# A graph-network kernel whose order is planned in Python: other durations and an occupancy in the planner, other buffers for the second sort, final rows kept in place

## The reference, cut to what matters

```python
x = _layernorm(x + _L0_gnn_ref(x, edge_attr_16, src, dst, ...))     # attention: softmax over a node's edges, sum of weighted rows
x = _layernorm(x + _L1_gnn_ref(x, edge_index, edge_weight, ...))    # attention, then normalise, MLP 64-128-64 with gelu, normalise
x = _layernorm(x + _L2_gnn_ref(x, edge_index, W, b))                # sums over src (row = src) of rows of dst, by degrees
x = _layernorm(x + _L3_gnn_ref(x, src, dst, edge_weight, 100000))   # sums over src of weighted rows of dst
```

## Time and profile before

| | us |
|---|---|
| median of three runs | 2920.24 |
| lowest, highest | 2912.45, 2922.75 |
| the profiled execution, device time | 2930.63 |
| its span in the profile | 2928.9 |
| PE busy | 2065.5 (71%) |
| POOL busy | 1644.4 (56%) |
| ACT busy | 1609.6 (55%) |
| DVE busy | 1599.0 (55%) |

### The profile page before, as it was taken

One profiled execution on the slowest core, in us unless ns is written; L12 is line 12 of the kernel. 1 busy time (PEld: TensorE's weight loads), 2 busy tenths in 40 slices (PEclk: granted clock), 3 DMA queues, 4 the chain that ended last, 5 costly groups with the idle time before them and its releaser, 6 DMA issues. The chain is left out here.

```text
span 2928.9 us, 28675 instructions
## 1 busy us (share of the span) xinstructions
PE 2065.5 (71%) x9124; PEld 1044.3 (36%) x9124; DVE 1599.0 (55%) x3043; ACT 1609.6 (55%) x2303; POOL 1644.4 (56%) x1609
## 2 busy tenths in 40 slices
PE   5888888878988889999999866578899840002221
PEld 2444333327543333654444354433333310002220
DVE  4776889983888778454443418964444420013331
ACT  3777666762568778457777724367777840001110
POOL 6777777300047761015665577757774027777776
PEclk9999988986999999889999956589999975555555
DMA  2223222211648862024443644421112100002220
GB/s 56 66 71 75 56 65 56 50 33 50 211 80 53 46 51 46 18 87 113 117 112 105 171 101 112 129 74 50 46 50 63 44 26 16 15 23 69 71 71 28
DMA packets 219596, 203.27 MB, mean 69 GB/s; under 512 B 144816, under 2 KB 157959, under 8 KB 219447
## 3 DMA queue, kind: packets, MB, share of 16 engines
q1 hardware_dynamic: 164998, 154.80, 18.6%
q0 software_dynamic: 51200, 46.31, 11.9%
q10 hardware_dynamic: 3248, 0.34, 0.1%
HBM read 134.59 MB, written 80.28 MB: 73 GB/s over the span
## 5 line engine op out<-in xcount | busy, mean ns | idle before, releaser
L854 PE MATMUL ps<-wk 127*64 127x125 f32 x1200 | 120.6, 366 | 458.0 <-DVE wk L839 457.0
L2217 POOL DMA_INDIRECT stab<-wk,rank_i x200 | 205.1, 1026 | 327.3 <-DVE wk L807 267.8
L509 ACT ACTIVATE b_s<-ps,vec 128x512 f32<-128x512 f32 (+1 forms) x444 | 296.2, 682 | 114.6 <-PE ps L506 71.7
L854 PEld LDWEIGHTS ps<-wk 127*64 127x64 f32 x1200 | 95.9, 190 | 480.9 <-DVE wk L839 476.2
L2214 POOL DMA_INDIRECT u<-x2tab,dpos_i x200 | 221.4, 1107 | 81.9 <-issue 76.7
L884 ACT ACTIVATE e_a<-ps 128x500 f32<-128x500 f32 x75 | 43.8, 584 | 398.3 <-PE ps L854 397.7
L2214 POOL DMA_INDIRECT u<-x3tab,src_i x200 | 204.8, 1024 | 89.3 <-issue 58.6
L2214 POOL DMA_INDIRECT e_b<-x0tab,dpos_i x72 | 72.4, 1006 | 309.9 <-DVEq L2018 287.2
L2214 POOL DMA_INDIRECT u<-in_x_dram,dst_i x200 | 205.5, 1028 | 63.6 <-issue 57.5
L2214 POOL DMA_INDIRECT u<-in_x_dram,src_i x200 | 197.8, 989 | 76.6 <-issue 57.2
L494 PE MATMUL ps<-b_h,blk_c 128*128 128x512 f32 (+1 forms) x296 | 175.4, 677 | 89.6 <-ACT b_gl L517 88.7
(11 more groups left out here) (422 smaller groups left out, 5296.6 us busy)
## 6 DMA issues: line engine op xcount, KB each, us to landing
b_gl<-in_x_dram SPq DMA_DIRECT2D x98, 256.0 KB, 2.8
out_dram<-b_gl SPq DMA_DIRECT2D x98, 256.0 KB
wk<-dlist SPq DMA_DIRECT2D x50, 500.0 KB
wk<-slist SPq DMA_DIRECT2D x50, 500.0 KB
u<-stab SPq DMA_DIRECT2D x25, 510.0 KB
x2none<-b_gl SPq DMA_DIRECT2D x25, 250.0 KB
wk<-x2none SPq DMA_DIRECT2D x25, 240.0 KB
x2tab<-wk SPq DMA_DIRECT2D x25, 240.0 KB
```

Source lines behind the costliest of these rows:

```text
L509: return nc.scalar.activation(b_s[l][:, 0:w], pB[l][:, 0:w], ACT.Abs_reciprocal_sqrt, bias=col(EPSV))
L854: last_a = nc.tensor.matmul(e0[64 * (k % 2):64 * (k % 2) + 64, P * (k // 2):P * (k // 2) + P], msg[n % 2][0:P + 2, D * k:D * k + D], sr[n ...
L2217: pool.indirect_dma_start(out=tab, out_offset=at(ix), in_=a, in_offset=None, bounds_check=rows_n - 1, oob_is_err=False).then_inc(s, 16)
```

## The change: planner, sort buffers and final rows

**Planner.** The durations of the steps are replaced by others: PE's steps of the lanes by shorter ones (1.3 to 1.15, 1.2 to 1.13), a group of eight indirect transfers by 10.5 to 11.2, some of DVE's and ACT's by a tenth or less. An engine is now free before a step's result is there: by 0.27 us on PE, 0.1 on ACT, 0.08 on DVE, but it stays occupied for at least 0.6 of the duration. The times of the index program in `IX` are set closer (the second sort from 424 to 602 instead of 462 to 690, its ticks 1.0 instead of 1.31). Two new units stand for the state of the index program: `packed` (the keys of the second sort are made and the four lists before it stored) and `ordered` (the sort is done). The units of layer 0 depend on the first, `prep2` 0 on the second.

**Second sort.** It works in `w_[11]`, `w_[9]`, `w_[10]`, which lie in `rec`, not in `msg`. SP raises `index_out` a first time after the packing; the messages and edge loads of layer 0 wait for that one, `prep2` for the second.

**Final rows.** The ring of three tiles is gone. The "only" rows of groups 0 to 2 go to `e_b`, `e_c` and a part of `rec[1]` (`staged`). Those of the other 22 groups are multiplied in place in `rdst` by a new step `own`, after the layer 3 message of the same group has read `rdst`. The `src` rows are written in place into `rsrc`. The squares of layer 3 use `e_d` alone. Layer 3's units no longer wait for `only` of the last group. POOL scatters in the order of `FINAL`: all `only` groups, then all `src` groups, as before.

```diff
+        OVERLAP = dict(pe=.27, act=.1, dve=.08)
...
                 done = t + us
-                free[eng] = done
+                free[eng] = t + max(us - OVERLAP.get(eng, 0.0), .6 * us)
...
-        MLP = ("w1 pe 1.3;gelu act 1.1;w2 pe 2.1;sq3 act .7;j3 pe 1.2;r3 act .7;mt dve .75;d pe 1.2;v dve .75;sq4 act .65;"
+        MLP = ("w1 pe 1.15;gelu act 1.1;w2 pe 2.1;sq3 act .7;j3 pe 1.13;r3 act .7;mt dve .75;d pe 1.13;v dve .75;sq4 act .63;"
...
+        STAGED = 3
+        FINAL = [("only", g) for g in GROUPS] + [("src", g) for g in GROUPS]
...
+        unit(("packed", 0), 0, f"t sp {IX['sort2'] + 8}")
+        unit(("ordered", 0), 0, f"t sp {IX['end'] - IX['sort2']}", [(("packed", 0), "t", 0)])
         for g in GROUPS:
-            unit(("u1", g), 0, "t pool 12.2", [(("u1", g - 1), "t", 0)] if g else ())
+            unit(("u1", g), 0, "t pool 10.5", [(("u1", g - 1), "t", 0)] if g else ())
...
-                      [(("lay", 3), "copy", CARRIED if g == 0 else 0), (("only", NG - 1), "t", 0)] +
-                      ([(("main", n - 2), "fin", 0)] if g >= 2 else []), sq=ring_free,
+                      [(("lay", 3), "copy", CARRIED if g == 0 else 0)] + ([(("main", n - 2), "fin", 0)] if g >= 2 else []),
...
+            unit(("final", p), 0, "t pool 10.6", [(("final", p - 1) if p else ("u6", NG - 1), "t", 0), step] +
+                 ([(("dense", NBLK - 1 - k), "out", STORED) for k in range(NL)] if p == 0 else []))
...
+            yield IX["sort2"] + 4
+            sp.wait_ge(S("index_made"), 3)
+            sp.wait_ge(S("q_st"), 64)
+            sp.sem_inc(S("index_out"), 1)
             yield IX["end"] + 1
-            sp.wait_ge(S("ordered"), 1)
+            sp.wait_ge(S("index_made"), 4)
...
-        pair = [w_[5], w_[6], w_[7]]
+        pair = [w_[11], w_[9], w_[10]]
...
+        def staged(g):
+            return (e_b[:, :], e_c[:, :], rec[1][:, 512:1024])[g]
...
+        def own_dve(dve, t, g):
+            a = rdst[0:P, GC * g:GC * g + GC, :]
+            yield t["own"]
+            nc.vector.tensor_tensor(a, a, bc(grp(r6c, g), D), ALU.mult).then_inc(S("only_rows"), 1)
...
-            dve.wait_ge(*ringed(NG + g - 3))
-            nc.vector.tensor_tensor(t3(ring[(NG + g) % 3][0:P, :]), rdst[0:P, GC * g:GC * g + GC, :], bc(grp(r6c, g), D),
-                                    ALU.mult).then_inc(S("final_rows"), 1)
+            nc.vector.tensor_tensor(t3(staged(g)[0:P, :]), rdst[0:P, GC * g:GC * g + GC, :], bc(grp(r6c, g), D),
+                                    ALU.mult).then_inc(S("only_rows"), 1)
...
-            act.wait_ge(*ringed(NG + slot - 3))
-            nc.scalar.activation(ring[(NG + slot) % 3][0:P, :], (q_a, q_b)[g % 2][0:P, :], ACT.Square).then_inc(S("src_sq"), 1)
+            act.wait_ge(S("src_var"), NG + slot)
+            nc.scalar.activation(e_d[0:P, :], (q_a, q_b)[g % 2][0:P, :], ACT.Square).then_inc(S("src_sq"), 1)
```

More of the change, by code:

```diff
@@ L222, in gnn_resnorm_kernel @@
         MAIN_A = "msg dve .7;same dve 1.2;"
-        MAIN_B = "sum pe 1.8 +e0;copy act .6 -e0;rows pe 1.1 +e1;"
+        MAIN_B = "sum pe 1.4 +e0;copy act .6 -e0;rows pe 1.2 +e1;"
         PREP2 = "a dve 1.8;rs act .5;b dve .5;p pe 2.4 +e0 +e1;c dve 1.6 -e0 -e1;q pe .5 +e0;d dve .4 -e0"
@@ L241, in gnn_resnorm_kernel @@
         for g in GROUPS:
-            sums_unit(g, MAIN_A + MAIN_B + "out dve .75 -e1;add dve .75", [(("lay", 0), "copy", CARRIED if g == 0 else 0)],
+            sums_unit(g, MAIN_A + MAIN_B + "out dve .75 -e1;add dve .75", [(("lay", 0), "copy", CARRIED if g == 0 else 0), (("packed", 0), "t", 0)],
                       **(dict(out=[(("main", g - 2), "out", STORED)]) if g >= 2 else {}))
-        unit(("prep2", 0), 1, PREP2, [(("lay", 0), "copy", 4.0)], a=[])
+        unit(("prep2", 0), 1, PREP2, [(("lay", 0), "copy", 4.0), (("ordered", 0), "t", 4.0)], a=[])
         for g in GROUPS:
@@ L298, in in_turn @@
                 for name in only or steps:
-                    steps[name][5].append(((kind, n - 1), name, 0))
-        for kind in ("l0", "l0d", "xd1", "x1s", "only"):
+                    if name in prev:
+                        steps[name][5].append(((kind, n - 1), name, 0))
+        for kind in ("l0", "l0d", "xd1", "x1s"):
             in_turn(kind, 0, NG)
@@ L1749, in index_dve @@
             stt(key, gi, 31, key, ALU.logical_shift_left, ALU.bitwise_or)
-            s1 = yield from sort(srt[0], srt[1], srt[2], 1.05)
+            s1 = yield from sort(srt[0], srt[1], srt[2], 0.95)
             bits = s1.bitcast(i32)
@@ L2278, in _ @@
                 pool.wait_ge(S(f"rows_st{l}"), 16 * before(l, len(lane_jobs[l]), dense=1, src=1))
-            for n in range(2 * NG):
-                pool.wait_ge(S("final_rows"), n + 1)
+            for kind, g in FINAL:
+                pool.wait_ge(S("only_rows" if kind == "only" else "src_rows"), g + 1)
                 pool.sem_inc(S("pool_turn"))
-                ix = (fidx_i, sfin_i)[n // NG]
                 for k in range(GC):
-                    b = GC * (n % NG) + k
-                    scatter(out, N, ix[:, b:b + 1], ring[(NG + n) % 3][:, D * k:D * k + D], ringed(NG + n)[0])
+                    b = GC * g + k
+                    if kind == "src":
+                        rows, ix = rsrc[:, b, :], sfin_i
+                    else:
+                        rows, ix = rdst[:, b, :] if g >= STAGED else staged(g)[:, D * k:D * k + D], fidx_i
+                    scatter(out, N, ix[:, b:b + 1], rows, S("final_st"))
         @block.tensor
```

99 lines of the change are left out of this document (54 added, 45 removed).

## The result

The changed kernel takes 2986.49 us (median of four runs, 2974.53 to 2996.95), the kernel before 2921.49 us (2912.45 to 2931.81) on the same chip. The ratio is 1.0222, 95% interval 1.0194 to 1.0251: 65 us slower, where 43 us faster was forecast. The profiled execution took 2982.83 us, its span 2981.1.

A forecast was written before the change was run, and what follows sets the result against it. Bound: storing the last dense block, then 528 us of POOL scatters. A chain 107 us shorter and dense blocks at 10.9 us, against 125 us of layer 3 messages, start the scatters 43 us earlier: about 2877 us, range 2775 to 2965.

The forecast's parts named there:

- The loads and layer 2's ends between these two ... stay: Between dst stage and layer 2's messages: loads and ends keep their length, as do the 269 us of u6 gathers.
- Softmax 0: Layer 0's scores, added at 617.3 us, come earlier as dot products follow their gathers: 46 us, bounds 0 to 71 less 4.
- Source stage: The 70 us between the u3 gathers and softmax 1 shrink as fewer xd1 groups are left over: 25 us, bounds 0 to 60.
- Dst stage: The 377 us stage with PE busy 346 shortens as PE starts steps closer together: 27 us, bounds 0 to 86.
- Layer 2's messages: The 199 us with DVE busy 170 become shorter: 9 us, bounds 0 to 29.
- Sort in its own buffers: Layer 0's first message no longer waits for the sort's end: 0 by itself, but lets softmax 0's 46 us be kept.
- Dense pace: Time per dense block beside the u6 gathers falls from 12.2 to 10.9 us, the middle between that and ACT's 9.5.
- C: Theory of the experiments: planned figures without slack put steps ahead of gathers they read, so PE stands at its queue's head.
- Layer 3 in front of the dense blocks: Layer 3's messages move from under the scatters to before the last dense blocks: costs 125 us, with 3 blocks done meanwhile.
- Tail unchanged, 528 us: The 400 final scatters on POOL show no wait, so they stay at 1.32 us each, 528 us.
- Rival 1: Layer 3 before the dense blocks outweighs the order: 3016 us if no order improves, about 2947 with half; slower 0.18.
- Rival 4: The port: DVE's 110 us in the tail hold up scatters and now fall away, giving 2767 us; chance 0.01.

The follow-up runs named there:

- e1: The changed kernel, with each matmul step of the ends stages allowed to follow the one before without a gap on PE: 2912.9 us, ratio 0.9975 to the kernel before.
- e10: e8 with the final rows going through the ring of three tiles, as in the kernel before: 2842.8 us, ratio 0.9700 to the kernel before.
- e6: The kernel before with only the planner's occupancy and the ends' steps chained without the gap: 2861.2 us, ratio 0.9782.
- e5: e1 with the third layer's u gathers (u6) planned at 12.6 us a group instead of 10.8: 2899.2 us, ratio 0.9912 to the kernel before.
- e8: e1 with all of GpSimd's planned gather figures as before (12.2, 12 and 12.6 us a group): 2866.7 us, ratio 0.9817 to the kernel before.
- e11: e1 with only the u3, u4 and u5 gathers at the old planned figures: 2881.1 us, ratio 0.9828 to the kernel before.
- e7: e1 with layer 3's main units ranked behind the dense blocks: 2900.2 us, ratio 0.9929 to the kernel before.
- e3: The changed kernel with layer 3's message units ranked behind the dense blocks, nothing else: 2976.5 us, ratio 1.0155 to the kernel before.
- e4: The kernel before with the planner's occupancy deductions alone: 2912.5 us, ratio 0.9957.
- e12: The changed kernel with 150 adds (both inputs in SBUF), then 150 reductions, added on DVE beside the scatters: 3002.8 us, ratio 1.0247 to the kernel before.

## Why the prediction was wrong, by its steps

**The step that failed: "The loads and layer 2's ends between these two ... stay", and with it the ends of layers 0 and 1, which the sum left out.** The cost of the occupancy was sought in the dense stretch alone. In the ends 25 steps of one engine hang on one another, and there a result that comes after the engine is free leaves a gap. They went from 39, 40 and 43 us to 76, 71 and 86: 111 us more, of which closing the gap gives 74 back in the end (e1, where 9 dense blocks instead of 7 are left behind u6).

- *Softmax 0*: 46 us forecast, 12.5 came. The forecast needed the second sort to be put off behind the scores, and it was not: of DVE's 56.8 busy us from 546 to 605, 40 are steps of the sort (lines 1652 to 1709) and 10 the dot products, and the sort's last cast is at 612 us, 17 earlier than before. In the plan its steps stand at fixed times, now 424 to 602.
- *Source stage*: 25 forecast; from the first message to softmax 1 it was 467 us before and 471 after, nothing gained. *Dst stage*: 27 forecast, 8 came (377 to 369 us; 16 in e1). *Layer 2's messages*: 9 forecast, 19 came (199 to 180 us, first message to first u6 gather), but nothing in e1 (201), where 5 dense blocks instead of 3 began between layer 2's ends and the u6 gathers.
- *Sort in its own buffers*: 0 by itself. No run did it alone; e10 differs from e6 by it, by the index program's plan and by durations, and has 0.8 points less.
- *Dense pace*: 10.9 us forecast, 12.9 came. (The sum took 265 us for this stage, which its rows give as 269: 0.4 block.) e5 and e8 show that PE's wait for gathers is not all of it: with that wait down to 8 us and under it is still 267/23 = 11.6 and 267/21 = 12.7. What the occupancy gains is blocks placed in the chain: counted by the same DVE instruction, e6 begins 16 between the last u2 and the first u3 gather where before has 12, and 8 between the start of layer 2's ends and u6 where before has 4.
- *GpSimd's planned figures*: the sum gave them a gain in softmax 0 and the source stage and no price. They cost 46 us (e1 against e8), two thirds or more of it in u3 to u5 (e11); the wait that C names is shown for u6 alone.
- *Layer 3 in front of the dense blocks*: 125 us forecast with 3 blocks in it. In the hole of 125 us 7 blocks ran together with layer 3, 17 of whose 25 groups had their message made before the first scatter: DVE 101 of 125 us, PE 101, ACT 92. Taking it away gives 13 to 20 us (e7, e3).
- *Tail unchanged, 528 us*: 535. POOL is busy in it as long as before (405.0 and 405.8 us). What grew is its idle time between scatters: its waits in the tail of the kernel after, and then of before, where the last hole of 154.2 is counted in (us in total, times, longest):

```profile
POOL out_dram L2244 <- issue: 129.6, 399, 3.0
```

```profile
POOL out_dram L2217 <- issue: 275.5, 399, 154.2
```

So 129.6 us against 121.3. The 8 us are three waits of 3.0 us, where the others are 0.3; they stand in every run with the final rows in place, and in none with the ring (before, e4, e6, e10). What makes them no run tests.

Rival 1 had the right side and the wrong cause. Rival 4 was put aside by a misreading: the two stretches of the earlier trace rows are alike because both have long scatters. DVE's 6% in the first are the products for the "only" rows, with both inputs in SBUF:

```profile
2405.37 0.69 DVE L1478 TENSOR_TENSOR e_c<-u,r5c 125x512 f32<-125x512 f32 x1 [16.14 <-DMA out_dram<-e_c,dst_i]
2405.68 1.24 POOL L2217 DMA_INDIRECT out_dram<-e_d,dst_i  x1 [0.31 <-issue]
```

Each stretch has 8 scatters of over 1.02 us, 2 and 3 us in excess. In the whole tail of before there are 42 in 400, each beside a DVE instruction with both inputs in SBUF, 13 us in excess: the effect is real, at an eighth of the 110 us of rival 4. The change did not win them back: its first four groups, beside the end of layer 3, took 15.2, 12.6, 12.6 and 12.1 us where 10.3 is the rule, 11 us in excess.

The terms as measured, by the ratios: the gap in the ends 2.5 points, GpSimd's figures 1.6, final rows in place 1.2 (e8 against e10), and the rest of the change (occupancy, other durations, sort buffers) -3.0; together 2.2, before rounding. They are taken off in this order; in another the shares can differ.

## What to carry to other kernels

When a planner learns that an engine is free before a result is there, look for chains of steps on one engine: any slack that it sees between them is filled with something else, and the chain pays for it. Durations without slack did not make a better plan here; put the head of each queue beside the transfers that it waits for. And price a move by the whole: a block moved from the hole into the chain cost 9 to 12 us there and gave back 15 to 18 behind it, less what the scatters lost.

## What the hardware showed that was not expected

A DVE instruction with both inputs in SBUF stretches POOL's issue of an indirect scatter beside it. In e12 75 scatters that began during such an add took 1.15 us in the mean, 78 that began during a reduction 0.98, and 210 with DVE idle 0.98. In e8 22 that began as the 127x1000 comparison started took 2.01, and the first scatter of the kernel after, with four such instructions in a row beside it, took 4.15. An add with one input in PSUM does nothing (0.98 in e8 and after). A mean over a stretch hides the effect, as in the earlier trace rows: it shows when each scatter is set against the instruction beside it. The Trainium skill, page "SBUF — State Buffer", section "Who interferes with whom", says that such a `tensor_tensor` contends with GpSimd's reads alone and infers that it leaves the writing of descriptors free; here the issue of a scatter was 0.17 to 1.03 us longer in the mean beside it, so that inference does not carry over to an indirect scatter. The scatter's record also names `dst_i`, the row numbers in SBUF, among what it reads; whether it is held at that read or at the writing of descriptors no run here tells. That a `tensor_reduce` never contends, as the same section has it, agrees.
